# GpSimd takes the second norm and the expert slots; VectorE's routing is spread over other steps

## The reference, cut to what matters

```python
xn = _layernorm(x)
x = x + _L0_attn_ref(xn, ...) + _L0_ffn_ref(xn, ...)
xn = _layernorm(x)                       # the second norm
x = x + _L1_attn_ref(xn, ...) + _L1_ffn_ref(xn, ...)
...
# L0_attn: relative position tables for keys and values
score = einsum('bhqd,bhkd->bhqk', q, k) + einsum('bhqd,qkd->bhqk', q, pe_k)
attn = softmax(score)
ctx = einsum('bhqk,bhkd->bhqd', attn, v) + einsum('bhqk,qkd->bhqd', attn, pe_v)
...
# L1_ffn: 16 experts, two for each token, with a capacity per expert
logits = x2d @ router_w.T + router_b
vals, idx = top_k(logits, 2)
gates = softmax(vals)
pos = cumsum(one_hot(idx)) - 1           # place of the token within its expert
kept = pos < capacity
gates = where(kept, gates / (sum(gates * kept) + 1e-9), 0)
slot = where(kept, idx * capacity + pos, dump)
buf[slot] = x2d                          # the rows that each expert computes on
```

## Time and profile before

| | us |
|---|---|
| median of 3 runs | 2618.43 (2608.91 to 2622.31) |
| the profiled execution | 2614.03 |
| its span, first to last instruction | 2612.1 |
| VectorE busy in the span | 1924.0 (74%) |
| TensorE busy in the span | 2249.0 (86%) |
| GpSimd busy in the span | 842.2 (32%) |

### The profile page before, as it was taken

How to read it: one execution, slowest core, us unless ns; L and a number is a source line. 1 busy time by engine, 2 the same in 40 slices (tenths; PEclk the granted TensorE clock), 3 DMA queues, 4 the chain that set the end, 5 groups by cost and what they waited for, 6 DMA issues and landing times. The chain is left out here.

```text
span 2612.1 us, 86943 instructions
## 1 busy us (share of the span) xinstructions
PE 2249.0 (86%) x32420; PEld 1793.6 (69%) x32420; DVE 1924.0 (74%) x7678; ACT 1717.8 (66%) x5582; POOL 842.2 (32%) x911
## 2 busy tenths in 40 slices
PE   5999998898888898888888888799986888787888
PEld 4888886677777777777777765577874555555555
DVE  6777773777778777877877866588875777676777
ACT  2333331887777777776777778566656777787778
POOL 3566665031111111111111122221116444545451
PEclk9999998999999999999999998799997999999999
DMA  7867542776676666766766730223211001111110
GB/s 196 235 173 187 118 108 64 188 181 169 168 177 171 166 169 165 174 168 162 175 166 164 176 96 20 81 96 113 103 68 33 26 24 26 32 26 32 26 30 12
DMA packets 361046, 304.53 MB, mean 117 GB/s; under 512 B 25656, under 2 KB 329144, under 8 KB 359240
## 3 DMA queue, kind: packets, MB, share of 16 engines
q1 hardware_dynamic: 350152, 271.93, 41.1%
q0 software_dynamic: 10496, 27.28, 3.5%
HBM read 166.43 MB, written 132.69 MB: 115 GB/s over the span
## 5 line engine op out<-in xcount | busy, mean ns | idle before, releaser
L871 ACT ACTIVATE probs<-neg_scores,low 128x256 f32<-128x256 f32 (+1 forms) x1152 | 574.2, 501 | 145.7 <-DVE low L1007 113.4
L1007 DVE CUSTOM_DVE_ANT_0 neg_scores<-scores,rel_bias 128x256 f32<-128x256 f32 x1024 | 373.3, 420 | 183.7 <-PE scores L1176 135.9
L1741 DVE CUSTOM_DVE_ANT_0 neg_scores<-scores,alibi 128x128 f32<-128x128 f32 (+1 forms) x896 | 265.9, 352 | 137.7 <-remote 77.3
L1188 PE MATMUL probsT<-consts,probs 128*128 128x128 f32 x2240 | 323.4, 288 | 7.4 <-issue 4.1
L1166 PE MATMUL scores<-k_heads,q_heads 32*128 32x256 f32 (+1 forms) x2304 | 211.1, 430 | 100.9 <-DVE rel_s L1015 66.9
L1703 ACT ACTIVATE probs<-neg_scores,low 128x128 f32<-128x128 f32 (+1 forms) x448 | 199.7, 447 | 137.9 <-DVE low L1741 123.8
L1188 PEld LDWEIGHTS probsT<-consts,probs 128*128 128x128 f32 x2240 | 251.2, 146 | 41.5 <-issue 13.7
L887 ACT COPY probsT_s<-probsT 128x512 f32<-128x512 f32 x288 | 167.2, 581 | 162.9 <-PE probsT L1188 138.2
L290 POOL TENSOR_TENSOR hid<-hid,gate_bc 128x512 f32<-128x512 f32 x160 | 205.6, 1289 | 157.0 <-DVE hid L482 149.1
L1015 DVE COPY rel_s<-scores 128x768 f32<-128x768 f32 x256 | 243.8, 953 | 6.5 <-PE scores L1176 5.1
L823 POOL TENSOR_SCALAR q_heads<-q_raw,consts,q_bias 128x256 f32<-128x256 f32 x128 | 69.2, 553 | 553.7 <-ACT q_raw L854 553.6
(11 more groups left out here) (216 smaller groups left out, 5131.8 us busy)
## 6 DMA issues: line engine op xcount, KB each, us to landing
rel_rows<-rel_s SPq DMA_DIRECT2D x256, 192.0 KB
rel_bias<-rel_rows SPq DMA_DIRECT2D x256, 192.0 KB
gate_bc<-gate_rows SPq DMA_DIRECT2D x32, 1024.0 KB, 10.7
rel_rows<-rel_s SPq DMA_DIRECT2D x256, 128.0 KB
rel_bias<-rel_rows SPq DMA_DIRECT2D x256, 128.0 KB
packed<-ffn_in SPq DMA_DIRECT2D x8, 1280.0 KB, 15.5
xe<-packed SPq DMA_DIRECT2D x16, 640.0 KB, 4.0
expert_out<-ye POOLq DMA_DIRECT2D x16, 640.0 KB, 3.2
```

The lines of the kernel that those rows point to most:

```text
L871: act.activation(probs[s % 3][:, j, 0:w], neg[s % 2][:, j, 0:w], ACT.Exp, bias=low[s % 3][:, j:j + 1], scale=-1.0, accum_out=sums[s // UB ...
L1007: dve.tensor_tensor_reduce(neg[s % 2][:, j, 0:w], S_ps[:, 512 * j:512 * j + w], bias_of(s)[:, j, :] if s < NU0 else alibi[:, 4 * j + s % 4 ...
L1188: ins = pe.transpose(PT_ps[kt][:, j * P:(j + 1) * P], probs[u % 3][:, j, kt * P:(kt + 1) * P], ident)
L1741: dve.tensor_tensor_reduce(neg[s % 3][:, j, 0:w], S_ps[j][:, 0:w], alibi[:, 4 * j + i, S - w:S], 1.0, 3e38, ALU.add, ALU.min, low[s % 3][: ...
```

## The change

The Newton steps and the writing of `xn2` go from VectorE to GpSimd (`normalise`), as do the slots (`slots`, whose reduction over 16 experts becomes four halving sums there). A Newton step is written in four instructions there and not three, and the slot's multiply and add are two. VectorE keeps statistics and moments (`normal_stats`, `normal_moments`), now in steps 6 and 7 of the odd batch, the copy of the counts (`prefix`, step 5), and the two largest (`top_two`, even step 6). The expert numbers move one step on (`places`, even step 7), the gates to odd step 1, the weights to step 1 of the next even batch. The scatters move with their own order on GpSimd: they stand in front of the next slots, in the even batch, and are held by units 8b+1 to 8b+4 of it.

```diff
+            moments_known = semm("second_norm_moments")
+            norm_steps = semm("second_norm_steps")
+            slot_steps = semm("slot_steps")
+            weights_known = semm("slot_weights_known")
...
+                v, y, a, c = nw[:, 0, :], nw[:, 1, :], nw[:, 2, :], nw[:, 3, :]
+                norm_count, slot_count = [0], [0]
+
+                def norm_step(ins):
+                    norm_count[0] += 1
+                    ins.then_inc(norm_steps, 1)
+                    pool.wait_ge(norm_steps, norm_count[0])
+
+                def slot_step(ins):
+                    slot_count[0] += 1
+                    ins.then_inc(slot_steps, 1)
+                    pool.wait_ge(slot_steps, slot_count[0])
+
+                def normalise(p):
+                    pool.wait_ge(moments_known, p + 1)
+                    for _ in range(3):
+                        norm_step(pool.tensor_tensor(a, y, y, ALU.mult))
+                        norm_step(pool.tensor_tensor(c, a, v, ALU.mult))
+                        norm_step(pool.tensor_scalar(c, c, -0.5, 1.5, ALU.mult, ALU.add))
+                        norm_step(pool.tensor_tensor(y, c, y, ALU.mult))
+                    if p >= 2:
+                        pool.wait_ge(scattered, 128 * (p - 1))
+                    for i in range(TP):
+                        ins = pool.tensor_scalar(xn2[p % 2][:, i, :], residual[:, TP * p + i, :], mv[:, i, 0:1], y[:, i:i + 1],
+                                                 ALU.subtract, ALU.mult)
+                    ins.then_inc(xn2_done, 1)
+
+                def slots(p):
+                    pool.wait_ge(spare_free, job_no["prefix", p])
+                    if p >= 1:
+                        pool.wait_ge(weights_known, p)
+                    slot_step(pool.tensor_tensor(pos[:, :, :], before[:, 0:TP, :], counts[:, :].unsqueeze(1).to_broadcast((P, TP, E)), ALU.add))
+                    slot_step(pool.tensor_tensor(counts[:, :], counts[:, :], before[:, TP, :], ALU.add))
+                    slot_step(pool.tensor_tensor(posk[:, :, :, :], oh[:, :, :, :], pos[:, :, :].unsqueeze(2).to_broadcast((P, TP, 2, E)), ALU.mult))
+                    n = E // 2
+                    while n >= 1:
+                        slot_step(pool.tensor_tensor(posk[:, :, :, 0:n], posk[:, :, :, 0:n], posk[:, :, :, n:2 * n], ALU.add))
+                        n //= 2
+                    slot_step(pool.tensor_scalar(kept[:, :, :], posk[:, :, :, 0], float(cap), None, ALU.is_lt))
+                    slot_step(pool.tensor_scalar(slot[:, :, :], idx[:, :, :], float(cap), None, ALU.mult))
+                    slot_step(pool.tensor_tensor(slot[:, :, :], slot[:, :, :], posk[:, :, :, 0], ALU.add))
+                    slot_step(pool.tensor_tensor(sk[:, :, :], slot[:, :, :], kept[:, :, :], ALU.mult))
+                    slot_step(pool.tensor_copy(slot_ids[:, TP * p:TP * (p + 1), :], sk[:, :, :]))
+                    slot_step(pool.tensor_tensor(dumpk[:, :, :], dump_at[:, :, :], kept[:, :, :], ALU.mult))
+                    slot_step(pool.tensor_tensor(dumpk[:, :, :], dump_at[:, :, :], dumpk[:, :, :], ALU.subtract))
+                    pool.tensor_scalar(dump_at[:, :, :], dump_at[:, :, :], float(TP * P), None, ALU.add).then_inc(slots_done, 1)
                     pool.wait_ge(slots_done, p + 1)
                     if p >= 1:
                         pool.wait_ge(scattered, 128 * p)
                     pool.tensor_tensor(scat_f[:, :, :], dumpk[:, :, :], sk[:, :, :], ALU.add).then_inc(rows_known, 1)
                     pool.wait_ge(rows_known, 2 * p + 1)
                     pool.tensor_copy(scat[:, :, :], scat_f[:, :, :]).then_inc(rows_known, 1)
-                    pool.wait_ge(rows_known, 2 * p + 2)
...
                 query_heads(0)
+                pool.wait_ge(started, 1)
                 for b in range(nb + 5):
                     if b + 1 < NB0:
                         query_heads(b + 1)
                     if b == 2:
                         for h in range(H):
                             pool.tensor_scalar(alibi[:, h, :], cview["distance"], float(SLOPES[h]), None, ALU.mult).then_inc(alibi_built, 1)
-                    p, odd = divmod(b - 5, 2)
-                    if odd == 0 and 0 <= p < nb // 2:
-                        rows_of(p)
+                    if b >= 6 and b % 2 == 0:
+                        p = (b - 6) // 2
+                        pool.wait_ge(rows_known, 2 * p + 2)
                         for i in range(TP):
                             for k in range(2):
-                                pool.wait_ge(lowest, 4 * min(NU0, UB * b + 6 + i))
+                                pool.wait_ge(lowest, 4 * min(NU0, UB * b + 2 + i))
                                 pool.indirect_dma_start(
                                     out=packed, out_offset=bass.IndirectOffsetOnAxis(ap=scat[:, i, k:k + 1], axis=0),
                                     in_=xn2[p % 2][:, i, :], in_offset=None).then_inc(scattered, 16)
+                    if b >= 5 and b % 2 == 1:
+                        slots((b - 5) // 2)
+                    if b >= 3 and b % 2 == 1 and (b - 3) // 2 < nb // 2:
+                        normalise((b - 3) // 2)
...
                 def normal_stats(p):
+                    if p >= 1:
+                        dve.wait_ge(xn2_done, p)
                     for i in range(TP):
                         ins = dve.bn_stats(stats[:, i, :], residual[:, TP * p + i, :])
                     link(ins)
 
-                def normal_begin():
+                def normal_moments():
                     for i in range(TP):
                         ins = dve.bn_aggr(mv[:, i, :], stats[:, i, :])
                     link(ins)
-                    link(dve.tensor_scalar(v, mv[:, :, 1], EPS, None, ALU.add))
-                    link(dve.tensor_scalar(a.bitcast(I32), v.bitcast(I32), 1, None, ALU.logical_shift_right))
-                    link(dve.tensor_scalar(y.bitcast(I32), a.bitcast(I32), -1.0, float(MAGIC), ALU.mult, ALU.add))
-
-                def newton():
-                    link(dve.tensor_tensor(a, y, y, ALU.mult))
-                    link(dve.scalar_tensor_tensor(c, a, -0.5, v, ALU.mult, ALU.mult))
-                    link(dve.scalar_tensor_tensor(y, c, 1.5, y, ALU.add, ALU.mult))
-
-                def normal_end(p):
-                    if p >= 2:
-                        dve.wait_ge(scattered, 128 * (p - 1))
-                    for i in range(TP):
-                        ins = dve.tensor_scalar(xn2[p % 2][:, i, :], residual[:, TP * p + i, :], mv[:, i, 0:1], y[:, i:i + 1],
-                                                ALU.subtract, ALU.mult)
-                    ins.then_inc(xn2_done, 1)
...
+                def places(p):
+                    if p >= 1:
+                        dve.wait_ge(slots_done, p)
                     for i in range(TP):
                         ins = dve.max_index(i8[:, i, :], m8[:, i, :], logit[:, i, :])
...
-                def slots(p):
-                    n = job_no["prefix", p]
-                    dve.wait_ge(spare_full, n)
+                def prefix(p):
+                    dve.wait_ge(spare_full, job_no["prefix", p])
+                    if p >= 1:
+                        dve.wait_ge(slots_done, p)
                     dve.tensor_copy(before[:, :, :], M_ps[:, 0:(TP + 1) * E].rearrange("p (t e) -> p t e", e=E)).then_inc(spare_free, 1)
-                    dve.wait_ge(spare_free, n)
-                    link(dve.tensor_tensor(pos[:, :, :], before[:, 0:TP, :], counts[:, :].unsqueeze(1).to_broadcast((P, TP, E)), ALU.add))
-                    dve.tensor_tensor(counts[:, :], counts[:, :], before[:, TP, :], ALU.add)
-                    link(dve.tensor_tensor(posk[:, :, :, :], oh[:, :, :, :], pos[:, :, :].unsqueeze(2).to_broadcast((P, TP, 2, E)), ALU.mult))
-                    link(dve.tensor_reduce(pk[:, :, :], posk[:, :, :, :], AX.X, ALU.add))
-                    link(dve.tensor_scalar(kept[:, :, :], pk[:, :, :], float(cap), None, ALU.is_lt))
-                    link(dve.scalar_tensor_tensor(slot[:, :, :], idx[:, :, :], float(cap), pk[:, :, :], ALU.mult, ALU.add))
-                    if p >= 1:
-                        dve.wait_ge(rows_known, 2 * p)
-                    link(dve.tensor_tensor(sk[:, :, :], slot[:, :, :], kept[:, :, :], ALU.mult))
-                    dve.tensor_copy(slot_ids[:, TP * p:TP * (p + 1), :], sk[:, :, :])
-                    link(dve.tensor_tensor(dumpk[:, :, :], dump_at[:, :, :], kept[:, :, :], ALU.mult))
-                    link(dve.tensor_tensor(dumpk[:, :, :], dump_at[:, :, :], dumpk[:, :, :], ALU.subtract))
-                    dve.tensor_scalar(dump_at[:, :, :], dump_at[:, :, :], float(TP * P), None, ALU.add).then_inc(slots_done, 1)
...
                 def slot_weights(p):
+                    dve.wait_ge(slots_done, p + 1)
...
                     p = (b - 3) // 2
                     if b >= 3 and b % 2 == 1 and p < nb // 2:
-                        if r == 3:
```

(16 more changed lines are left out.)

12 lines of the change are left out of this document (6 added, 6 removed).

## The result

| | before | after |
|---|---|---|
| median of 20 runs each, us | 2619.2 (2607.3 to 2630.8) | 2605.9 (2596.6 to 2614.6) |
| ratio after/before | | 0.9956, 95% interval 0.994 to 0.9971 |
| the profiled execution, us (its span) | 2614.0 (2612.1) | 2614.6 (2612.9) |

The change makes the kernel 0.44% faster. The forecast was 2551 us, 2.6% faster, and the time lies 6 us above its range. The profiled execution of after is the slowest of its twenty, so the two profiles show the same span; what they are good for is where the time stands.

A forecast was written before the change was run, and what follows sets the result against it. It took VectorE's routing, with TensorE near it and scatters stalling TensorE, to bound the kernel. From 2614.0 us it took 62.8 and 8 for routing and added 8 for the moved scatters: 2551 us, range 2475 to 2600.

The forecast's parts named there:

- What bounds the kernel: First attention: VectorE's routing lengthens steps of 3.58 us, 4.9 us a pair; scatters add 6.9 us a pair.
- The routing's term: Routing chains leaving VectorE's steps save 4.4 us a pair, 62.8 us, plus 8 us in the second attention's four batches.
- GpSimd: Moved slots and norm cost GpSimd 9.5 us a pair, and nothing of its work reaches the path.
- The rival in which GpSimd becomes the bound: Late norm on GpSimd delays query heads and TensorE's scores in even step 3; 2640 us at four times cost, chance 0.06.
- Where the stall stands: TensorE's unexplained gaps in even steps 3 to 5, lower clock behind them, a certain pause before the seventh scatter.
- How large it is: The moved scatters' stall of TensorE in the even batch: 7.4 us a group against 6.9, 8 us more over 16 groups.
- the prediction's own 1.33: Factor on the stall's lost time for lower clock and echo, from batch 15's 5.2 reckoned against the pair's 6.9 us.
- 0 to 2 for the last two: Extra us a group for the last two scatters, which now follow 2 to 3 us behind the stall instead of 7.5.
- The case without one: Eight scatters without a pause at batch 31, where TensorE got 24 matmuls in 8.7 us.
- The stall grows: Scatters' new place, even batch: stall of 11 to 12 us a group, 2617 us; at 10 us 2593; chance 0.12.
- The stall goes away: Scatters in the new place cost TensorE under 2 us a group, about 2450 us; chance 0.16.
- Sum: Whole kernel: 2614.0 less 62.8 and 8 for routing, plus 8 for moved scatters, gives 2551 us.

The follow-up runs named there:

- after_none: The changed kernel with its 128 scatters of xn2 and the waits for them left out; 2439.1 us, ratio 0.935 to the kernel before.
- before_none: The kernel before the change with its 128 scatters of xn2 and the waits for them left out; 2510.7 us, ratio 0.9598.
- after_direct: The changed kernel with each scatter replaced by a plain DMA of the same block from GpSimd's queue to a fixed place; 2458.7 us, ratio 0.9399.
- the singles: The changed kernel with scatters held one to a step, in all 36 batches for the pair of 59.78 us; that version took 2451.9 us, ratio 0.9394.

## Why the prediction was wrong, step by step

**What bounds the kernel.** Right for the steps it spoke of: odd steps 3 to 6 and even step 6 fell to 3.6 to 3.7 once VectorE's routing was gone, and odd step 7 to 3.8 in the mean. With them quiet, what shows is TensorE, and that the forecast had left out: even steps 0 and 1 take 4.08 and 3.70 in after_none instead of 3.71 and 3.58 in before_none, odd steps 0 and 1 4.06 and 3.70 instead of 3.82 and 3.58, together 0.85 us a pair. Even step 7, 4.02 instead of 3.67, is mostly VectorE's own moved work, forecast at 3.9. The busy table of batch 14's step 7 and batch 15's step 0, in before_none and in after_none:

```profile
916.90:924.35 7.45, 6.42 (x179) 5.39 (x172) 6.47 (x26) 5.29 (x18) 0.00 (x0) 1.00 0.76 188
```

```profile
898.52:906.53 8.01, 7.87 (x247) 6.70 (x246) 7.31 (x34) 5.70 (x21) 0.00 (x0) 1.00 0.87 231
```

In the second TensorE is busy 7.87 of 8.01 us; of these step 7 took 3.90, without idle time on VectorE, and step 0 4.11, with a wait of 0.45 us for TensorE's `projected`. VectorE's waits for TensorE between 640 and 1340 us (us in total, times, longest) tell the same of the latter, first before_none, then after_none:

```profile
DVE ctx_all L1055 <- PE projected L1109: 2.1, 11, 0.2
```

```profile
DVE ctx_all L1086 <- PE projected L1137: 6.7, 19, 0.7
```

The routing's term was 4.4 a pair and 62.8 + 8 us in all; it measured 3.42 and 54.1, with 9.6 of it in batches 31 to 35. This is 17 of the 54 us by which the steps' sum was off at the experts' start.

**GpSimd.** Right. Slots and rows take 910.51 - 905.12 = 5.4 us (forecast 5.0); the norm 919.86 - 913.32 = 6.5 (4.5), as the four xn2 take 0.79 us each, where I had put 0.35 from q_heads' 0.54. The query heads begin 3.00 us later, by ScalarE's copy. Between 500 and 1510 us TensorE never waits for q_heads, and GpSimd's busy time is 331 us (forecast 340). The rival in which GpSimd becomes the bound is out. VectorE's work beside GpSimd's instructions did not lengthen them either. The row has the first Newton instruction of each of 48 steps (ns, least, median and most): 30 of them ran wholly while VectorE was busy and 7 while it was idle, with 197 to 201 ns for all. The query heads' 116 took 544 to 563 ns.

```profile
L830 POOL TENSOR_TENSOR nw<-nw x48: 197/198/201, 575.5 to 1591.4; 128x4 f32<-128x4 f32 x48
```

**Where the stall stands.** Right: even steps 3 and 4, six scatters, a certain pause before the seventh, gaps without a semaphore, the lower clock (0.50) behind them, none of it in odd step 7. Step 4, with the last two scatters and what the stall leaves behind, takes 1.3 us more than in after_none.

**How large it is: the step that failed.** "Until about 8.6 us TensorE gets 45 + 6.3 x (2.8 to 6.1) = 63 to 83 matmuls", so 7.4 us a group against 6.9. It got 57 in 8.9 us: 39 up to the first gap, which came after 1.07 us and not after 2.3, and behind it 2.4 a microsecond:

```profile
925.19:926.26 1.07, 1.07 (x39) 0.71 (x32) 0.24 (x1) 0.89 (x3) 1.07 (x1) 1.00 0.69 139
...
926.26:934.09 7.83, 2.67 (x19) 1.55 (x18) 2.10 (x9) 0.60 (x2) 4.83 (x6) 0.71 0.81 217
```

57 are 2.8 us of work at the 20.6 a microsecond of the earlier trace rows, so 6.1 lost; with the prediction's own 1.33 and 0 to 2 for the last two that is 8.2 to 10.2, and 9.97 was measured. The mechanism held, the supply did not; the factor and the term for the last two can't be told apart in the sum, but steps 2 and 3 alone grew by 8.8 over after_none, which is 1.4 times 6.1. I had read it from batch 15, whose scatters are four, a pause of 1.38, two, and the last two 7.5 us later: 17 of its 35 matmuls run as one group that starts at 987.95, in that pause, 0.28 us ahead of the fifth scatter. A row of six has no such pause. The case without one was in the rows, 24 in 8.7 us at batch 31, and I had weighed it as the lower end. The scatters were reckoned at 8 us more in all; at the experts' start they are 45 us more. That is 37 of the 54 us. The range was also added up too narrowly: its own ends (4 to 14, and 4 to 10 us a group) give 2491 to 2597 and not 2500 to 2590, still below what was measured.

**The rivals.** "The stall grows" (10 us a group: 2593; 11 to 12: 2617) is what happened. It named as its reason that TensorE has no idle time there; but a row of eight costs 11.1 and three 4.4 in the same place, so the row's length counts too; no run has a row of six in the old place. "The stall goes away" is wrong for after, but after_direct and the singles show that it can: pairs of 59.59 and 59.78 us, and TensorE 15.51 of 16 us busy beside single scatters. Nor do TensorE's gaps go with transfers of instructions. The page of the profile of after has these transfers as two queues (transfers, MB, share of the DMA engines):

```profile
q8 instruction: 252, 4.13, 0.7%
q14 instruction: 147, 1.20, 0.1%
```

In the first attention each of q8 took 0.87 to 1.92 us. In batch 14 one of them ran from 925.41 to 927.16 and the next of either queue from 937.89, and neither belongs to the return of the stream at 934.09. In batch 12 none ran from 854.08 to 862.99, and all its gaps but the last, from 856.04 on, lie in that time; its first gap came 1.09 us behind the first scatter, as in batch 14, where a transfer was under way. So TensorE is held up while no transfer of instructions is recorded. What connects the issuing of indirect DMAs with TensorE's gaps stays open.

**Sum.** Forecast -62.8 - 8 + 8; by the experts' start -54.1 + 45.2 = -8.9 us; the medians differ by 13.3.

## What to carry to other kernels

Count how many indirect DMAs GpSimd issues without a pause, not how many there are: alone, a step (3.6 us) or more apart, they cost TensorE nearly nothing here, and a group of eight with six or all of them in a row 10 to 11 us where TensorE is full. Hold each by its own semaphore count, check that the work queued ahead of them on GpSimd does not end so late that several holds are already met, and that the holds don't run out at the loop's end. When a stall is read from a trace and carried to another place, read the supply from the stretch whose spacing the new place will have.

## What the hardware showed that I had not expected

- The cost of scatters by the length of their row: alone next to nothing (0.3 us for eight), two 0 to 0.9, three 3.9 to 4.4, six and two 10.0, eight 11.1. From six and two to eight it hardly grows. Between two and three it seems to jump, but the couples stood in other steps than the threes, so the place may have a part in it; no run has two in even step 3.
- Rows and bytes do not matter to it: 32 rows a scatter cost what 128 do (a pair of 69.85 against 69.43). A plain DMA of GpSimd's queue takes 0.56 us to issue (2.24 for four), an indirect one 0.96 and 0.30 between two.
- GpSimd's xn2 takes 0.79 us for 128 elements and its query heads 0.55 for 256, though both are one instruction with two per-partition scalars.
- The rest of the program, which no kernel here changes, takes 938 to 965 us, 92 to 149 of them at the lower clock level, 0.50. So differences of 10 us between medians are to be read at the experts' start, and not from the whole.
